# Mixing stage of a three-block kernel: which engine prepares the norms, when the router's choice is made, and how routed rows are sent

## Time and profile before

| what | value |
|---|---|
| median of 3 runs | 312.11 us (311.23 to 314.89) |
| profiled execution: its own time | 313.16 us |
| profiled execution: span from first to last instruction | 311.4 us |
| mean granted TensorE clock | 0.971 |
| PE busy | 281.0 us, 90% of the span |
| DVE busy | 240.4 us, 77% |
| POOL busy | 239.4 us, 77% |
| ACT busy | 182.9 us, 59% |

### The profile page before, as it was taken

The page is one execution under the profiler, slowest core; times in us unless marked ns, Lnnn a source line. Parts: engine busy times, 40 slices in busy tenths (PEclk is TensorE's granted clock), DMA queues, the critical chain, the costliest instruction groups (busy, mean ns, idle before and its releaser), DMA issues.

```text
span 311.4 us, 7732 instructions
## 1 busy us (share of the span) xinstructions
PE 281.0 (90%) x2177; PEld 245.2 (79%) x2177; DVE 240.4 (77%) x1014; ACT 182.9 (59%) x543; POOL 239.4 (77%) x330
## 2 busy tenths in 40 slices
PE   7999999986899999999998996987899999999950
PEld 7666676665698999999954785965798999999950
DVE  4888999997787877777717998879977977777740
ACT  3776666522598866666604762723498876666620
POOL 4759388887778888888746857788878888888760
PEclk9999999998999999999999997999799999999995
DMA  6998610001514544321018001011412454321000
GB/s 184 251 345 203 68 38 28 26 28 44 123 47 104 116 94 122 90 65 42 17 50 220 3 1 35 29 43 35 114 55 74 126 109 114 94 74 44 29 6 1
DMA packets 32522, 25.64 MB, mean 82 GB/s; under 512 B 6000, under 2 KB 28785, under 8 KB 32480
## 3 DMA queue, kind: packets, MB, share of 16 engines
q1 hardware_dynamic: 27328, 16.51, 22.8%
q0 software_dynamic: 4576, 8.54, 8.4%
q10 hardware_dynamic: 576, 0.10, 0.2%
HBM read 14.57 MB, written 11.53 MB: 84 GB/s over the span
## 4 chain that ended last, share of the span: by engine, by line
PE 57%; DVE 24%; POOL 6%; issue 5%; ACT 2%; DMA 2%; POOLq 0%; DVEq 0%; SPq 0%
PE pair L1618 20%; PE pair L1604 15%; PE bank L1604 6%; DVE stats L817 3%; POOL sorted L499 3%; PE bank L1594 3%; PE pair L1482 2%; PE pair L1382 2%; DVE zT L1032 2%; PE pair L1474 2%; DVE sc L1091 2%; DVE rows L954 1%; POOL rows L473 1%; PE pair L1441 1%; PE pair L1387 1%
## 5 line engine op out<-in xcount | busy, mean ns | idle before, releaser
L1618 PE MATMUL pair<-w2s,hT 128*128 x624 | 82.5, 276 | 0.4 <-issue 0.4
L499 POOL DMA_INDIRECT sorted<-rows,place x64 | 65.8, 1028 | 19.6 <-issue 15.3
L1618 PEld LDWEIGHTS pair<-w2s,hT 128*128 128x128 f32 x624 | 75.6, 192 | 0.8 <-issue 0.8
L1604 PE MATMUL pair<-xsT,w1s 128*128 128x128 f32 x432 | 60.8, 278 | 0.9 <-ACT xsT L756 0.9
L1604 PEld LDWEIGHTS pair<-xsT,w1s 128*128 128x128 f32 x432 | 54.7, 194 | 1.6 <-issue 1.0
L679 ACT COPY w1s<-w1all 128x516 f32 x78 | 49.5, 635 | 2.9 <-DVE etab L1178 1.9
L1250 DVE SCALAR_TENSOR_TENSOR ys<-pair,xs 128x128 f32<-128x128 f32 x78 | 27.2, 349 | 26.6 <-PE pair L1618 26.0
L519 POOL DMA_INDIRECT x_mid<-ys,xs x39 | 39.2, 1006 | 8.3 <-issue 5.2
L519 POOL DMA_INDIRECT out<-ys,xs x39 | 39.2, 1006 | 8.3 <-issue 5.1
L756 ACT COPY xsT<-bank 128x128 f32<-128x128 f32 x78 | 20.8, 267 | 41.9 <-PE bank L1594 41.2
L1240 DVE TENSOR_SCALAR hT<-pair,w1s 128x128 f32<-128x128 f32 x112 | 34.5, 346 | 1.4
(11 more groups left out here) (168 smaller groups left out, 522.3 us busy)
## 6 DMA issues: line engine op xcount, KB each, us to landing
xs<-sorted SPq DMA_DIRECT2D x78, 66.0 KB, 2.0
w1all<-in_L_ffn_W_b SPq DMA_DIRECT2D x8, 258.0 KB, 5.7
rows<-in_L_attn_a_x SPq DMA_DIRECT2D x8, 256.0 KB, 4.0
w2s<-in_L_ffn_W SPq DMA_DIRECT2D x8, 256.0 KB, 6.3
rows<-x_mid SPq DMA_DIRECT2D x8, 256.0 KB, 4.5
sorted<-pad SPq DMA_DIRECT2D x30, 66.0 KB, 3.4
sorted<-rows,place POOLq DMA_INDIRECT x64, 2.4
x_mid<-ys,xs POOLq DMA_INDIRECT x39, 2.3
```

Source lines behind the costliest of these rows:

```text
L499: pool.indirect_dma_start(sorted_rows[l], bass.IndirectOffsetOnAxis(ap=place[:, t:t + 1], axis=0), rows[:, t, :], None).then_inc(s_sent[l] ...
L1604: mm = nc.tensor.matmul(bank[2 + 2 * half + i % 2][:, c * P:(c + 1) * P], w1s[i % NW][:, f:f + P], xsT[i % NB][:], start=True, stop=True)
L1618: mm = nc.tensor.matmul(bank[6 + i % 2][:, 0:P], hT[i % NB][:, c], w2s[:, bass.ds(e, 1), c, :].rearrange("p o d -> p (o d)"), start=(c == ...
```

## The change

It does the following, in this order of the diff:

- `MIX_NORM_BATCHES` joins groups 4 and 5.
- `COUNT_AT`, `PLACE_AT` and `TABLE_AT` go from 5, 5, 7 to 7, 7, 9, in both layers.
- The sends of the mixing stage follow a table, `SENDS_OF_MIX`: four tiles in each of the slots 3 to 6 ahead of the power, in slot 7 four behind it, in slot 8 four ahead of it and four behind.
- `pause` is issued in the first 26 iterations of the experts alone (`LAGS`).
- SP's waits between the layers run in the order in which the scatters are issued.
- In layer 1 the negative mean and the epsilon of the first moments are made by DVE inside `first_moments`, and POOL is left with the power and the product.
- In mixing, DVE's choice and the moments of the next group are interleaved (`choose_and_measure`), `first_moments` stand one to three places earlier, and on ACT `evac_x2T` goes ahead of `row_veps`.
- On PE `count` goes behind the second half of `mix_scan`.
- The last group's mix, its moments, its transposes on PE and its copy on ACT go ahead of the first expert tile.

The core of the diff:

```diff
-MIX_NORM_BATCHES = [[0], [1], [2], [3], [4], [5], [6, 7]]
+MIX_NORM_BATCHES = [[0], [1], [2], [3], [4, 5], [6, 7]]
-CHOOSE_AT, COUNT_AT, PLACE_AT, TABLE_AT = 3, 5, 5, 7
+CHOOSE_AT, COUNT_AT, PLACE_AT, TABLE_AT = 3, 7, 7, 9
-PAUSE = 320
+SENDS_OF_MIX = [(range(a, b), range(b, c)) for a, b, c in
+                ((0, 0, 0), (0, 0, 0), (0, 0, 0), (0, 4, 4), (4, 8, 8), (8, 12, 12), (12, 16, 16), (16, 16, 20),
+                 (20, 24, 28))]
+PAUSE, LAGS = 320, 26
...
-                for b in range(ND):
-                    sp.wait_ge(s_sct[b], ring_total(l + 1, b, ND))
+                for i in range(ST - ND, ST):
+                    sp.wait_ge(s_sct[i % ND], ring_total(l + 1, i % ND, ND))
...
                 for i in range(ST):
-                    pause(next(pauses))
+                    if i < LAGS:
+                        pause(next(pauses))
                     scatter(l, i)
...
-            for b in range(5):
+            for b in range(4):
                 scales(BS, b)
             for k in range(NG + 1):
-                if 0 <= k - 1 < LASTB:
+                if k == 1:
+                    scales(BS, 4)
+                if k == 2:
+                    scales(BS, 5)
+                send_tiles(1, BS, SENDS_OF_MIX[k][0])
+                if 0 <= k - 1:
                     row_scales(BS, k - 1)
-                if k == 1:
-                    scales(BS, 5)
-                if k == 3:
-                    scales(BS, 6)
-                if k == NG:
-                    send(1, BS, k - 2, 0)
-                    row_scales(BS, LASTB)
-                    send(1, BS, k - 2, 1)
-                elif k - 2 >= 0:
-                    send(1, BS, k - 2)
+                send_tiles(1, BS, SENDS_OF_MIX[k][1])
...
             def first_moments(l, g):
                 dve.wait_ge(s_x_in[g], 16 * (l + 1))
                 moments((AS, BS)[l], 1, g)
+                if l == 1:
+                    t = tiles(g)
+                    dve.wait_ge(BS["st1"], 2 * g + 2)
+                    nc.vector.tensor_scalar(nmean1[:, t], mv1[:, t, 0], -1.0, None, ALU.mult)
+                    nc.vector.tensor_scalar(veps1[:, t], mv1[:, t, 1], EPS, None, ALU.add).then_inc(BS["ve1"], 1)
...
+            def choose_and_measure(b, g):
+                dve.wait_ge(BS["xnew"], g + 1)
+                row_stats(BS, g, 0)
+                scale_logits(1, BS, b)
+                row_stats(BS, g, 1)
+                bias_logits(1, BS, b)
+                row_stats(BS, g, 2)
+                max_logit(1, b)
+                row_stats(BS, g, 3)
+                lead_logits(1, BS, b)
+                dve.wait_ge(BS["st2"], 2 * g + 1)
+                row_moments(BS, g, 0)
+                rank_leaders(1, BS, b)
+                row_moments(BS, g, 1)
+                top_rank(1, b)
+                row_moments(BS, g, 2)
+                one_hot(1, BS, b)
+                row_moments(BS, g, 3)
...
             def mix_slot(k):
                 if 0 <= k - 1:
                     add_mix(k - 1)
-                if k == NG:
-                    return
-                if k - 2 >= 0:
-                    choose(1, BS, k - 2)
-                if 0 <= k - 1:
+                if k == 1:
                     dve.wait_ge(BS["xnew"], k)
                     moments(BS, 2, k - 1)
+                if k - 2 >= 0:
+                    choose_and_measure(k - 2, k - 1)
                 if k + 1 < NG:
                     scan_mix(k + 1)
                 if k - 2 >= 0:
                     placed(1, BS, k - 2)
                 if k == 0:
-                    first_moments(1, 4)
+                    first_moments(1, 5)
+                    first_moments(1, 6)
                 if k == 1:
-                    first_moments(1, 5)
-                if k == 2:
-                    first_moments(1, 6)
                     first_moments(1, 7)
...
                 else:
+                    add_mix(LASTG)
+                    dve.wait_ge(S["xnew"], NG)
+                    moments(S, 2, LASTG)
                     norm_rows(0)
-                    add_mix(LASTG)
...
             first_moments(1, 2)
+            first_moments(1, 3)
             dve.wait_ge(s_decay, 2)
             scan_mix(0)
-            first_moments(1, 3)
+            first_moments(1, 4)
...
-                if 2 <= k < LASTG:
-                    count(BS, k - 2, bank[7])
                 if 0 <= k - 1:
                     transpose_x2(k - 1)
                 mix_scan(k, 1)
-                if k == LASTG:
+                if k >= 2:
                     count(BS, k - 2, bank[7])
...
+                if l == 1:
+                    transpose_x2(LASTG)
                 turn(0)
```

More of the change, by code:

```diff
@@ L255, in hybrid_block @@
                                                 "dmax rden lold lnew").split()}
-        BS = {n: sem(f"b_{n}") for n in BOTH + "scan mix sig vm x2T x2Te logits lnew".split()}
+        BS = {n: sem(f"b_{n}") for n in BOTH + "ve1 scan mix sig vm x2T x2Te logits lnew".split()}
         s_le = [sem(f"s_le{l}") for l in range(2)]
@@ L455, in scales @@
                 n = GT * len(groups)
-                pool.wait_ge(S["st1"], 2 * (groups[-1] + 1))
                 if S is BS:
[L458 to L466, removed]
+                    pool.wait_ge(BS["ve1"], groups[-1] + 1)
+                    nc.gpsimd.tensor_tensor(rstd1[:, t], veps1[:, t], neg_half[:, 0:n], ALU.pow).then_inc(BS["rs1"], 1)
+                    pool.wait_ge(BS["rs1"], 2 * b + 1)
+                    nc.gpsimd.tensor_tensor(nmr1[:, t], nmean1[:, t], rstd1[:, t], ALU.mult).then_inc(BS["rs1"], 1)
+                    return
+                pool.wait_ge(AS["st1"], 2 * (groups[-1] + 1))
+                nc.gpsimd.tensor_scalar(veps1[:, t], mv1[:, t, 1], EPS, None, ALU.add).then_inc(AS["rs1"], 1)
+                pool.wait_ge(AS["rs1"], 3 * b + 1)
+                nc.gpsimd.tensor_tensor(rstd1[:, t], veps1[:, t], neg_half[:, 0:n], ALU.pow).then_inc(AS["rs1"], 1)
+                pool.wait_ge(AS["rs1"], 3 * b + 2)
+                nc.gpsimd.tensor_tensor(std1[:, t], veps1[:, t], rstd1[:, t], ALU.mult).then_inc(AS["rs1"], 1)
             def row_scales(S, b):
@@ L529, in experts @@
             def experts(l):
-                pauses = itertools.count(l * (ST + GT))
+                pauses = itertools.count(l * (LAGS + GT))
                 for i in range(ST):
-                    pause(next(pauses))
+                    if i < LAGS:
+                        pause(next(pauses))
                     scatter(l, i)
@@ L604, in norm @@
                 b = batch_of(MIX_NORM_BATCHES if S is BS else NORM_BATCHES, g)
-                act.wait_ge(S["rs1"], 3 * b + (2 if S is AS else 3))
+                act.wait_ge(S["rs1"], 3 * b + 2 if S is AS else 2 * b + 2)
                 after(act, S["xT"], g - 1)
@@ L763, in relu @@
                     last.then_inc(s_rA, 1)
+                if l == 1:
+                    evac_x2T(LASTG)
+                    row_veps(BS, LASTB)
                 evac_xs(0)
@@ L779, in experts @@
                         lexp(l, (AS, BS)[l], LASTB - 1)
-                    if i == l:
-                        row_veps((AS, BS)[l], LASTB)
+                    if i == 0 and l == 0:
+                        row_veps(AS, LASTB)
                     if i == CHOOSE_AT + 1:
@@ L1070, in norm_half @@
             def norm_half(S):
-                dve.wait_ge(S["rs1"], 2)
+                dve.wait_ge(S["rs1"], 2 if S is AS else 1)
                 if S is BS:
@@ L1280, in experts @@
                         placed(l, S, LASTB - 1)
-                        dve.wait_ge(S["xnew"], NG)
-                        moments(S, 2, LASTG)
                     if i == 1:
@@ L1679, in _ @@
             keep_clock(2)
-            pe.wait_ge(BS["rs1"], 1)
+            pe.wait_ge(BS["ve1"], 1)
             keep_clock(2)
```

8 lines of the change are left out of this document (2 added, 6 removed).

## The result

On the same chips the changed kernel took 311.93 us (median of 20 runs, 310.54 to 313.27), the kernel before 314.13 (20 runs). The ratio is 0.9944 [0.9926, 0.9962]: 1.75 us (1.2 to 2.3) where 3.4 were forecast; the two medians by themselves lie 2.2 us apart. The 312.11 that the forecast counted from, a median of three runs, was 2 us low, so that of the 3.2 us between the forecast 308.7 and the measured 311.93 some 2.0 belong to the starting point. The profiled execution took 311.58 with a span of 309.8, against 313.16 and 311.4: 1.6 us, to be found in the stages.

The account below looks back on a forecast made before the run. PE was taken to bound the expert stages, DVE early mixing, POOL mixing from the first sends. Gains of 0.9 + 0.25 + 0.4 + 1.9 = 3.45 us from 312.11 gave 308.7 us, eight in ten between 306.4 and 311.6.

Parts of the forecast that it names:

- The count: Last group's count on PE, two iterations later: its wait for DVE's choice goes, 0.9 us in layer 0, 0.7 in layer 1.
- SP's waits and the pauses: Between the layers: reordered waits gain 0.25 us (0 to 0.37); dropping late pauses gains 0.2 in each layer.
- Mixing up to the sends: Layer 1's mixing: first send at 188.6 instead of 186.53, fourth group's sends at 208.0 instead of 210.34, 2.3 us earlier.
- The rival with the scans: Mixing: DVE's scans keep lengthening POOL's sends, 0.83 us more in each of three periods; 310.8 us, chance 0.24.
- From there to the first output were 4.72 us, in layer 0 3.54, since nothing stands between any more: Layer 1, tile 0's turn to first output: shortened to layer 0's time, so first output at 224.6 for 226.11, 1.5 us earlier.
- So the rows of tile 9 still decide: Layer 1's experts: tile 9's rows set the eighth output, 239.75 against 239.4 for PE alone; gain 1.9 us (-1 to 3.5).
- a fall of the granted clock in the expert tiles: Expert tiles: listed as a sign the forecast is wrong, if PE's granted clock falls with a step longer than 1.92 us.

Follow-up runs that it names:

- `lexp`: Changed kernel with ACT's exponential of the last group's logits one iteration later in both layers: 311.84 us, ratio 0.9929.
- `keep2`: Changed kernel with four unused products (two of 512 columns, two of 256) in PE's idle time in the last mixing slots: 310.0 us, ratio 0.989.
- `lastmix_alone`: Kernel before with only the last group's mix, moments and transposes moved ahead of the first tile: 318.04 us, ratio 1.0164.
- `pow6`: Changed kernel with group 4's sends ahead of the power of group 6 on POOL: 311.81 us, ratio 0.9933.
- `cnt_back`: Changed kernel with count, place and table of the last group back in iterations 5, 5 and 7: 313.25 us, ratio 0.9975.
- `lastmix_back`: Changed kernel with only the last group's mix, moments and transposes put back behind the first tile's: 309.93 us, ratio 0.9888.
- `back_rows`: Changed kernel with the last mix put back, group 4's sends ahead of group 6's power and group 6's ahead of group 7's: 308.83 us, ratio 0.9857.
- `best1`: `back_rows` and `lexp` together, with group 6's count and places ahead of layer 1's first output: 307.33 us, ratio 0.9813.
- `keep`: Changed kernel with seven unused 128x512 products on PE in gaps of the last mixing slots: 311.85 us, ratio 0.9923.
- `all5`: Changed kernel with the edits of `keep2`, `lexp` and `pow6`, and group 6's count and places ahead of layer 1's first output: 309.13 us, ratio 0.9866.
- `best2`: `best1` with two unused products (512 and 256 columns) in PE's idle times of the last mixing slot: 307.26 us, ratio 0.9803.
- `best3`: `best2` with group 6's count and places left behind layer 1's first output: 307.6 us, ratio 0.9794.

## Why the prediction was half right

Against the forecast the span came out 1.9 us long: 2.1 from the turn of tile 0 to the first output, 0.3 from the count in layer 0, 0.2 between the layers, 0.1 at the start, and 0.75 the other way in mixing.

- **The count: right, mis-sized.** 0.56 us came in layer 0 and 0.48 in layer 1, where 0.9 and 0.7 were forecast. The wait went, but its cover went too: DVE's choice still ends when it did, and ACT's exponential waits for it (`lexp`). The step looked at PE and DVE, not at who else waits for the choice.
- **SP's waits and the pauses: right.** The chain shows 0.21 at the last scatter and 0.29 at the load. 0.26 of 0.45 came between the layers, since the load itself took 2.98 in place of 2.83 (2.78 in `keep2`, where the stretch has the whole 0.46), and 0.23 at the end. Not tried apart.
- **Mixing up to the sends: right.** Layer 1 started 0.73 us earlier than before. First send 187.73 (188.6 less 0.73), the fourth group's at 206.94 (208.0 less 0.73), POOL's 3.03 us ahead of the power of group 6. The turn at 219.60 is 0.75 earlier than 221.1 less 0.73: 0.33 were there at the fourth group's sends, the rest came in DVE's work behind them, which the sum has too long (the power of group 6 starts at 215.96, where 217.5 less 0.73 was forecast). That this made up for what the count lacked is luck. The rival with the scans fell: after a first period of 6.94 us the groups' sends follow each other at 6.18 and 6.09, a scan in each. (The long send in the period from 203.36 is not the one at 212.94, which belongs to the next, but one at 205.97, of 1.85.)
- **"From there to the first output were 4.72 us, in layer 0 3.54, since nothing stands between any more": the step that failed.** It put the 1.2 us of difference down to the last group's transposes and took them as saved. In the kernel before, the first eight products took 2.05 us and the next 1.09: most of the difference was half clock, and that row was not read. Moving the last mix ahead empties PE further (3.13 of 6 us busy), the half clock lasts twice as long, and the term came out as 0.9 lost instead of 1.2 won. `keep2` puts the 2.1 us back by unused products alone; `lastmix_alone` shows the part by itself, 5.1 us slower, 2.67 of them the late turn. The profiles sort the same way: 6.8 us of half clock at this join in all five that have the last mix ahead and no unused products (the changed kernel, `pow6`, `lexp`, `cnt_back`, `lastmix_alone`), 3.4 in the four that have it behind and no products (the kernel before, `lastmix_back`, `back_rows`, `best1`), none in the three with it ahead and products (`keep`, `keep2`, `all5`). That more idle time makes the half clock longer is shown; how much idle time PE may have is not (`best2`, `best3`).
- **"So the rows of tile 9 still decide": wrong for this kernel, right for its neighbour.** Here tile 9 was ready 1.7 us before PE turned it, and in the kernel before 1.3 us. The rows decide once the mix is put back (`lastmix_back`, `back_rows`).
- What the text listed as a sign of error, a fall of the granted clock in the expert tiles, is what happened; it had no price and no chance among the rivals.

## What to carry to other kernels

Where a chain of hand-overs joins two stages, read the granted clock and the length of like instructions on both sides of it before putting a gap down to what stands in between: eight products at twice their length are not a wait. Work moved ahead of a busy stage must not leave TensorE idle there; if it does, either keep it where TensorE is busy, or fill the idle time, and no more than that. Where a wait of TensorE goes, half clock behind it may go too, and more is won than the wait. And when a wait is moved away, ask who else waits for the same thing.

## What the runs showed of the hardware

Up to the first output of layer 0 the fourteen kernels profiled here issue the same work, and it came between 82.80 and 84.92 us. The clock sorts them (granted clock from 73 to 83 us): 1.00 in three executions, 82.80 to 83.27; 0.83 in nine, 83.57 to 84.61; 0.66 in two, 84.75 and 84.92. So with the same instructions 0, 3.4 or 6.8 us of half clock were seen at that join, and each 3.4 us cost about one. The three at 1.00 are `lastmix_back`, `back_rows` and `best1`, which all have the last mix put back, an edit that stands far behind this place; whether that is chance stays open, and the spans of their profiles hold about a microsecond of it. In the change's 20 runs the span goes with the mean clock in the same way: 308.7 to 309.0 at 0.978, 311.1 to 311.5 at 0.970 and below. So a difference of a microsecond between two single executions of this kernel says nothing by itself.

A send that begins while DVE's scan runs is mostly lengthened by much of what is left of the scan. A send beside no such instruction takes 0.96 us (1.03 to 1.11 for the first of a group). In the kernel before, the sends 0.07 and 0.11 us into a scan took 1.97 and 1.85 (at 205.97); after the change the one at 190.72 begins with 0.65 us of a scan still to come:

```profile
190.18 1.19 DVE L1119 TENSOR_TENSOR_SCAN sc<-decay,xnT 128x512 f32<-128x512 f32 x1
```

```profile
190.72 1.43 POOL L504 DMA_INDIRECT sorted<-rows,place  x1 [0.30 <-issue]
...
202.19 0.96 POOL L504 DMA_INDIRECT sorted<-rows,place  x1 [0.30 <-issue]
```

The next scans end 0.3 us or less into a send, and these took 0.96 to 1.06; one that is under way when a scan starts (202.19, scan at 202.44) keeps its 0.96. So does one in the kernel before that begins 0.03 us behind the start of a scan:

```profile
198.59 1.28 DVE L1091 TENSOR_TENSOR_SCAN sc<-decay,sc,xnT 128x512 f32<-128x512 f32 x1
198.62 0.96 POOL L499 DMA_INDIRECT sorted<-rows,place  x1 [0.30 <-issue]
```

DVE's add of the rows does the same: the first send of mixing, at 187.73, begins with 0.48 us of an add still to come and takes 1.41. The Trainium skill ("GPSIMD Engine Reference", section "Specifications") states the contention with VectorE instructions that have two SBUF inputs, as the scan and this add have; the rows agree, but for the send at 198.62, and give its size: it depends on where in the scan the send begins.
